# Decoder block on one core: the cross-attention's two halves as one unrolled program

## The chip, the cores and the metric

The kernel runs on one core of one Trainium2 chip. The metric is device time in microseconds (us). Three runs of the kernel before gave 2765.36, 2766.39 and 2767.1 us; the median is 2766.39 us.

## The reference

The program is one decoder block for 32 batches of 112 tokens with 512 channels, all float32. It adds three sublayers to `x`, each fed with a layer norm of `x`: windowed self-attention, cross-attention to a context, and a mixture of eight experts. The change touches the second.

```python
# text 32 x 112 x 512, context 32 x 375 x 256, 16 query heads, 8 key/value heads of 128
q = (text @ Wq).reshape(B, 112, 16, 128)      # Wq 512 x 2048
k = (ctx @ Wk).reshape(B, 375, 8, 128)        # Wk 256 x 1024
v = (ctx @ Wv).reshape(B, 375, 8, 128)        # each k, v head serves two query heads
attn = softmax(mask(q k^T / sqrt(128)))
out = (attn v).reshape(B, 112, 2048) @ Wo     # Wo 2048 x 512
x = x + out
```

## The kernel before

The program is four stages one after the other, with a barrier between them: `window_attention` (self-attention, which also writes the normalised, transposed text `h2T`), `cross_attention` for half 0, `cross_attention` for half 1, and `expert_ffn`. A half is 8 query heads and 4 key/value heads. Half 0 adds its part of the output to `x1` and writes `x1_half`; half 1 adds to that and writes `x2`.

Each float32 matrix product is made of three products in the format fp32r: an operand is split into a high part (ScalarE copies it, rounding) and a low part (VectorE subtracts the high part from the source), and `PASSES` multiplies high by high, high by low and low by high. So every result that TensorE makes for a later product is emptied from PSUM twice, by ScalarE and then by VectorE.

The products that feed the attention are called fills, and each has a letter. C transposes 128 context channels of a batch. K makes the keys of one key head of a batch (6 matmuls of 376 columns). V makes the values of a batch for 128 context rows (6 of 512 columns, three V fills a batch). Q makes queries of two heads for two batches (two groups of 12 matmuls of 224 columns). O multiplies the attention output of a batch with Wo (24 matmuls of 512 columns, 112 rows of output). Fills go through three PSUM banks in turn.

A step is one key head of one batch, with its two query heads. A turn is two batches, so eight steps, and a half has 16 turns. The first and last turn are written out; the 14 between are a hardware loop (`Fori`) on each engine. The order of all work is written out by hand in the list `FULL`, which gives each of the eight steps some of the fills, so that the steps are alike in TensorE work: no step has fewer than two or three fills except the two that have an O. On TensorE (L1461 on) a step `s` is: scores of `s`, transposes of the normalised probabilities of `s-1`, an O fill if there is one, the product of probabilities and values (pv) of `s-2`, and the other fills.

The softmax of a step goes round the engines. VectorE adds the mask and takes the maximum (`maxima`, L1279), GpSimd makes the bias from it (L1127), ScalarE takes the exponential and the sum (`exps`, L1199), VectorE inverts the sum (`inverses`, L1305 and L1308), GpSimd multiplies the probabilities (L1135), TensorE transposes them (L1436), and ScalarE and VectorE split them into `pT` (`probsT`, L1177 and L1286), which has room for two steps. The pv result in the one bank `ps_o` is split into `oT` (`out`, L1184 and L1294). Every engine works strictly in its written order.

The weights are staged: each 128 x 512 piece is loaded into free room (`stage`, `probs`, `sums`), then split. The text of two batches is loaded into `xf` and split into `xT` in one piece (L1192, L1261). The SyncE queue issues all the loads and stores.

Of the kernel before, what the change touches and what calls it, by code (L numbers as in the profile page):

```python
# [16 lines left out]
P = 128  # L17
# [99 lines left out]
def window_attention(nc, B, T, x, Wq, bq, Wk, bk, Wv, bv, Wo, bo, x1, h2T, slots, rest):  # L117
# [45 lines left out]
    with ExitStack() as stack:  # L163
# [51 lines left out]
        blank_made, blank_out = sem("blank_made"), sem("blank_out")  # L215
        x1_out = [sem(f"x1_out{s}") for s in range(TB)]
# [32 lines left out]
        with nc.Block() as block:  # L249
# [3 lines left out]
            def _(sp):  # L253
# [99 lines left out]
                sp.wait_ge(blank_out, 16 * (TURNS + 2))  # L353
                for s in range(TB):
                    sp.wait_ge(x1_out[s], 16 * TURNS)
# [106 lines left out]
            def _(act):  # L462
# [392 lines left out]
def cross_attention(nc, half, B, T, S, h2T, ctx, mask, Wq, Wk, Wv, Wo, base, result):  # L855


# [12 lines left out]
    H = 2 * G  # L870
    SE = S + S % 2
# [3 lines left out]
    assert 0 < SE - S or S % 2 == 0  # L875
    T2 = 2 * T
    TURNS = B // 2
    SCALE = float(1.0 / np.sqrt(D))
    mdt = mask.dtype

    LATE = [("Q", 0, 3), ("K", 0, 3), ("V", 0, 1), ("V", 0, 2)]
    FULL = [
        [("Q", 0, 3), ("K", 1, 0), ("V", 0, 1)],
        [("K", 0, 3), ("V", 0, 2), ("K", 1, 1), ("V", 1, 0)],
        [("O", 0, 1)],
        [("K", 1, 2), ("C", 0, 0), ("V", 1, 1), ("C", 0, 1)],
        [("K", 1, 3), ("V", 1, 2), ("Q", 0, 0)],  # L890
        [("K", 0, 0), ("Q", 0, 1)],
        [("K", 0, 1), ("Q", 0, 2)],
        [("O", 1, 0), ("K", 0, 2), ("C", 1, 0), ("V", 0, 0), ("C", 1, 1)],
    ]
    HEAD = [f for f in [("C", 0, 0), ("C", 0, 1)] + [("K", 0, g) for g in range(G)] + [("V", 0, c) for c in range(NKC)] +
            [("C", 1, 0), ("C", 1, 1)] + [("Q", 0, g) for g in range(G)] if f not in LATE]
    FIRST = [[f for f in fs if f != ("O", 0, 1)] for fs in FULL]
    LAST = [[f for f in fs if f[0] == "O" or f in LATE or (f[0] in "KV" and f[1] == 1)] for fs in FULL]
    TAIL = [("O", 0, 1)]
    NF = sum(map(len, FULL))  # L900
    NF0 = sum(map(len, FIRST))
    BASE = len(HEAD) + NF0 - NF
    flat = [f for fs in FULL for f in fs]
# [3 lines left out]
    def fills_until(turn, fill):  # L907

        if turn.reg is None and turn.at == -1:
            return HEAD.index(fill) + 1  # L910
# [1191 lines left out]
```

## Time and profile before

| | |
|---|---|
| profiled execution, span | 2765.4 us |
| median of three runs | 2766.39 us |
| TensorE matmul busy | 2589.5 us (94%) |
| VectorE busy | 1755.7 us (63%) |
| ScalarE busy | 1294.8 us (47%) |
| GpSimd busy | 1032.2 us (37%) |
| self-attention stage | 0 to 462 us |
| cross-attention, half 0 | 462 to 1474 us |
| cross-attention, half 1 | 1474 to 2487 us |
| expert stage | to 2765.4 us |

Busy shares are averages over stages with different limits. Matmuls are pipelined, so the time from the start of one block of matmuls to the start of the next is a better price for a block than its printed length, which reaches into the next block.

### The profile page before, as it was taken

The page shows a single profiled execution, that of the slowest core. Times are in us where ns is not written, and L with a number is a line of the kernel's source. Part 1 is how long each engine was busy: PE and PEld are TensorE (multiplying, and loading weights), DVE is VectorE, ACT ScalarE, POOL GpSimd, SP SyncE. Part 2 cuts the span into 40 slices and gives each one's busy share as a digit, 9 for nine tenths or more (in the row PEclk, how much of TensorE's full clock was granted, in tenths as well). Part 3 has the DMA queues.
Part 4 walks back from the last instruction along what each step waited for, and adds up shares of the span by engine and source line. Part 5 has one row for each costly group of instructions (what it writes and reads, how often), then busy time and mean ns, then how long its engine had stood idle before and what let it go on. Part 6 is the DMA issues. An engine that isn't in the chain of part 4 may idle for free. (4 is left out here: it accounts for less than half of the span.)

```text
span 2765.4 us, 56399 instructions
## 1 busy us (share of the span) xinstructions
PE 2589.5 (94%) x16770; PEld 2364.0 (85%) x16771; DVE 1755.7 (63%) x4862; ACT 1294.8 (47%) x3135; POOL 1032.2 (37%) x1426
## 2 busy tenths in 40 slices
PE   6899996899999999999996999999999999988688
PEld 5888886899999999999986899999999999978576
DVE  7888886656666665666664666665666665555466
ACT  4555554545545454554543545454554554441211
POOL 4334433333344433333341444333334344332422
PEclk9999998999999999999998999999999999995599
DMA  3223224111111111111113111111111111103654
GB/s 101 89 72 100 89 94 141 53 37 45 32 32 38 42 32 36 44 34 32 32 30 115 30 33 44 36 32 36 45 32 32 37 43 32 34 16 110 228 173 126
DMA packets 122050, 168.80 MB, mean 61 GB/s; under 512 B 20753, under 2 KB 69329, under 8 KB 121857
## 3 DMA queue, kind: packets, MB, share of 16 engines
q1 hardware_dynamic: 116944, 151.43, 18.3%
q0 software_dynamic: 5040, 16.58, 1.5%
q8 instruction: 33, 0.54, 0.1%
q14 instruction: 33, 0.26, 0.0%
HBM read 111.73 MB, written 56.23 MB: 61 GB/s over the span
## 5 line engine op out<-in xcount | busy, mean ns | idle before, releaser
L1135 POOL TENSOR_SCALAR x_probs<-x_probs,x_inv 112x376 f32<-112x376 f32 x512 | 652.5, 1285 | 237.2 <-DVE x_inv L1308 237.2
L1127 POOL TENSOR_SCALAR x_bias<-x_top 112x1 f32<-112x1 f32 x512 | 117.9, 230 | 977.5 <-DVE x_top L1279 976.5
L1392 PE MATMUL x_ps_f<-x_wo,x_oT 128*112 128x512 f32 x1536 | 374.8, 400 | 1.9 <-DVE x_oT L1294 1.9
L1392 PE MATMUL x_ps_f<-x_xT,x_wq 128*128 128x224 f32 x3072 | 365.8, 275 | 7.0 <-DVE x_xT L1261 7.0
L1392 PEld LDWEIGHTS x_ps_f<-x_xT,x_wq 128*128 128x128 f32 x3072 | 361.8, 193 | 10.4 <-issue 7.4
L1199 ACT ACTIVATE x_probs<-x_probs,x_bias 112x376 f32<-112x376 f32 x512 | 308.1, 604 | 64.1 <-POOL x_bias L1127 57.8
L1392 PEld LDWEIGHTS x_ps_f<-x_wo,x_oT 128*112 128x112 f32 x1536 | 265.3, 176 | 85.0 <-issue 2.2
L1452 PE MATMUL x_ps_o<-x_pT,x_v 128*128 128x224 f32 (+1 forms) x2304 | 315.6, 282 | 2.7 <-DVE x_oT L1294 2.7
L1424 PE MATMUL x_ps_s<-x_kT,x_qT 128*112 128x376 f32 x1536 | 311.4, 338 | 5.4 <-DVE x_wo L1244 5.4
L1392 PE MATMUL x_ps_f<-x_ctxT,x_wk 128*128 128x376 f32 x1536 | 312.7, 340 | 2.5 <-DVE x_ctxT L1250 2.5
L1392 PE MATMUL x_ps_f<-x_wv,x_ctxT 128*128 128x512 f32 (+1 forms) x1152 | 304.9, 400 | 0.0
L1177 ACT ACTIVATE x_pT<-x_ps_t 128x336 fp32r<-128x336 f32 x512 | 204.0, 449 | 206.0 <-PE x_ps_t L1436 206.0
L1452 PEld LDWEIGHTS x_ps_o<-x_pT,x_v 128*128 128x128 f32 (+1 forms) x2304 | 284.0, 193 | 9.6 <-issue 3.4
L1279 DVE CUSTOM_DVE_ANT_0 x_probs<-x_ps_s,x_mrow 112x376 f32<-112x376 f32 x512 | 259.8, 543 | 19.4 <-DVE x_mrow L1266 17.2
L1392 PEld LDWEIGHTS x_ps_f<-x_ctxT,x_wk 128*128 128x128 f32 x1536 | 262.4, 193 | 6.2 <-issue 3.2
L1424 PEld LDWEIGHTS x_ps_s<-x_kT,x_qT 128*112 128x112 f32 x1536 | 253.7, 175 | 12.9 <-DVE x_wo L1244 5.7
L1286 DVE TENSOR_TENSOR x_pT<-x_ps_t,x_pT 128x336 fp32r<-128x336 f32 x512 | 235.4, 500 | 9.3 <-ACT x_pT L1177 7.1
L1392 PEld LDWEIGHTS x_ps_f<-x_wv,x_ctxT 128*128 128x128 f32 (+1 forms) x1152 | 208.7, 187 | 36.3
L1250 DVE TENSOR_TENSOR x_v<-x_ps_f,x_v 128x512 fp32r<-128x512 f32 (+1 forms) x192 | 132.7, 691 | 151.1 <-ACT x_v L1169 151.0
L1250 DVE TENSOR_TENSOR x_qT<-x_ps_f,x_qT 128x448 fp32r<-128x448 f32 x128 | 79.9, 624 | 225.8 <-ACT x_qT L1169 225.8
L1184 ACT ACTIVATE x_oT<-x_ps_o 128x224 fp32r<-128x224 f32 x256 | 87.8, 343 | 278.2 <-PE x_ps_o L1452 278.2
L1436 PE MATMUL x_ps_t<-x_ident,x_probs 112*128 112x112 f32 x1536 | 192.4, 260 | 11.0 <-POOL x_probs L1135 11.0
(194 smaller groups left out, 3876.0 us busy)
## 6 DMA issues: line engine op xcount, KB each, us to landing
x_ctxn<-in_ctx_dram SPq DMA_DIRECT2D x64, 256.0 KB
x_xf<-h2T SPq DMA_DIRECT2D x32, 448.0 KB, 4.2
m_rows<-slots SPq DMA_DIRECT2D x35, 258.0 KB, 2.9
slots<-w_blank SPq DMA_DIRECT2D x8, 1032.0 KB, 5.2
m_hn<-in_L_ffn_W_dram SPq DMA_DIRECT2D x32, 256.0 KB, 4.9
x_ctxn<-in_ctx_dram SPq DMA_DIRECT2D x64, 119.0 KB
w_xa<-in_x_dram SPq DMA_DIRECT2D x32, 224.0 KB, 3.0
w_xr<-in_x_dram SPq DMA_DIRECT2D x32, 224.0 KB, 3.2
```

The lines of the kernel that those rows point to most:

```text
L1127: pool.tensor_scalar(bias[:, m:m + 1], top[:, m:m + 1], -0.1 * NEG, -SCALE, ALU.max, ALU.mult) \
L1135: pool.tensor_scalar(probs[0:T, m, 0:SE], probs[0:T, m, 0:SE], inv[:, m:m + 1], None, ALU.mult).then_inc(normed, 1)
L1177: act.activation(pT[:, s % 2, HI, :, h * T:(h + 1) * T], ps_t[h][:, 0:NKC * T].rearrange("p (c t) -> p c t", c=NKC), ACT.Copy).then_inc(pT ...
L1184: act.activation(oT[:, HI, 2 * g:2 * g + 2, odd * T:(odd + 1) * T], ps_o[:, 0:T2].rearrange("p (h t) -> p h t", h=2), ACT.Copy).then_inc(o ...
L1199: act.activation(probs[0:T, m, 0:SE], probs[0:T, m, 0:SE], ACT.Exp, bias=bias[:, m:m + 1], scale=SCALE, accum_out=total[:, m:m + 1]).then_ ...
L1250: dve.tensor_tensor(dst[LO], src, dst[HI].bitcast(F32), ALU.subtract).then_inc(fill_done, 1)
L1279: dve.tensor_tensor_reduce(out=probs[0:T, m, 0:SE], in0=ps_s[h][0:T, 0:SE], in1=mrow[:, s // 4, :], scale=1.0, scalar=-3.0e38, op0=ALU.add ...
L1286: dve.tensor_tensor(pT[:, s % 2, LO, :, h * T:(h + 1) * T], ps_t[h][:, 0:NKC * T].rearrange("p (c t) -> p c t", c=NKC), pT[:, s % 2, HI, : ...
L1392: last = pe.matmul(o, w, x, start=m == 0, stop=m == len(jobs) - 1)
L1424: last = pe.matmul(ps_s[h][0:T, 0:SE], qT[:, a, 2 * g + h, odd * T:(odd + 1) * T], kT[:, b_, g, :], start=m == 0, stop=m == 2)
L1436: last = pe.transpose(ps_t[h][:, c * T:(c + 1) * T], probs[0:T, n % 4, c * P:(c + 1) * P], ident[0:T, 0:T])
L1452: last = pe.matmul(ps_o[:, 0:T2], w, x, start=m == 0, stop=m == len(jobs) - 1)
```

## The change

Both halves become one `cross_attention` call, with every step written out in the program and no hardware loop: 64 batches (32 for each half) of 4 steps, 256 steps.

- Q fills make one query head for four batches at once: 12 matmuls of 448 columns. All eight of a group of four batches are issued in the last batch of the group before, two in each step.
- O fills work on 128 consecutive tokens and not on one batch: 28 tiles a half, 24 matmuls of 512 columns each with 128 rows of output. `oT` is a ring of 256 tokens. An O fill is issued in the third step (g = 2) of the batch after the one with its last token. Four batches of each half have none.
- The split, transposed context of each batch in half 0 is also stored to device memory (`ctxs`, 32 pieces of 128 x 1504 float32) and in half 1 loaded from there, so half 1 has no C fills.
- The three V fills of a batch stand together in its second step (g = 1); `v` and `pT` have room for one batch and one step, where they had two.
- A K fill of the next batch stands in every step; in half 0 two C fills stand in the fourth step (g = 3).
- TensorE's step is now: scores of `i`, K, C and O fills, pv of `i-2`, V and Q fills, and last the probability transposes of `i-1`. ScalarE and VectorE split `pT` of `i-2` at the start of step `i`. ScalarE copies K and C before `exps`.
- The text is split in four pieces, one a step, in the second batch of each group of four. The weights are loaded straight into the low half of their tile and split there, in pieces of 128 x 512 or 128 x 1024; those of half 1 are split in steps of the running program.
- The four weight matrices are copied in device memory (`own`) by four DMAs, issued from ScalarE's queue ahead of the first turn of the self-attention.

```diff
-        [("Q", 0, 3), ("K", 1, 0), ("V", 0, 1)],
-        [("K", 0, 3), ("V", 0, 2), ("K", 1, 1), ("V", 1, 0)],
-        [("O", 0, 1)],
...
+    def early_fills(i):
+        b, g = divmod(i, G)
+        out = [("K", b + 1, g)] if b + 1 < NB else []
+        if g == 3 and b + 2 < B:
+            out += [("C", b + 2, 0), ("C", b + 2, 1)]
+        if g == 2 and b in TILE_OF:
+            out.append(("O", TILE_OF[b], 0))
         return out
+    def late_fills(i):
+        b, g = divmod(i, G)
+        out = [("V", b, c) for c in range(NKC)] if g == 1 else []
+        if b % QUAD == QUAD - 1 and b + 1 < NB:
+            out += [("Q", b // QUAD + 1, 2 * g + h) for h in range(2)]
+        return out
...
-        pT = sb("pT", [P, 2, 2, NKC, T2], F32R)
+        pT = sb("pT", [P, 2, NKC, T2], F32R)
...
+                def keep_ctxT(b):
+                    sp.wait_ge(fill_done, until(("C", b, 1)))
+                    sp.dma_start(ctxs[b], ctxT[:, b % 2].rearrange("p a c s -> p (a c s)").bitcast(F32)) \
+                        .then_inc(ctx_out[b % 2], 16)
...
+                for i in range(STEPS):          # VectorE
+                    if i >= 2:
+                        probsT(i - 2)
+                    if i % G == 0:
+                        mask_row(i // G)
+                    maxima(i)
+                    for p in splits_at(i):
+                        split(p)
+                    for f in early_fills(i):
+                        if f[0] != "O":
+                            fill(f)
+                    inverses(i)
+                    if x_piece(i) is not None:
+                        split_x(x_piece(i), i % G)
+                    for f in early_fills(i):
+                        if f[0] == "O":
+                            add(f)
+                    if i >= 2:
+                        out(i - 2)
+                    for f in late_fills(i):
+                        fill(f)
...
+                for i in range(STEPS):          # TensorE
+                    scores(i)
+                    for f in early_fills(i):
+                        fill(f)
+                    if i >= 2:
+                        pv(i - 2)
+                    for f in late_fills(i):
+                        fill(f)
+                    if i >= 1:
+                        probsT(i - 1)
...
+                for n, (dst, src) in enumerate(copies):
+                    act.dma_start(dst, src).then_inc(copied[n], 16)
...
-    for half, (base, result) in enumerate(((x1, x1_half), (x1_half, x2))):
-        cross_attention(nc, half, B, T, S, h2T, ctx_1024, mask, xattn_Wq, xattn_Wk, xattn_Wv, xattn_Wo, base, result)
+    cross_attention(nc, B, T, S, h2T, ctx_1024, mask, *own, x1, x1_half, x2)
```

## Rows read from the trace of the kernel before

**Rows 1.** The page: busy time by engine, and TensorE's granted clock in 40 slices.
```profile
PE 2589.5 (94%) x16770; PEld 2364.0 (85%) x16771; DVE 1755.7 (63%) x4862; ACT 1294.8 (47%) x3135; POOL 1032.2 (37%) x1426
PEclk9999998999999999999998999999999999995599
```

**Rows 2.** Timeline of TensorE, one turn: start us, length us, engine, line, operation.
```profile
1001.03 1.20 PE L1424 MATMUL x_ps_s<-x_kT,x_qT 128*112 128x376 f32 x6
...
1002.58 5.82 PE L1392 MATMUL x_ps_f<-x_wo,x_oT 128*112 128x512 f32 x24
1008.24 1.16 PE L1452 MATMUL x_ps_o<-x_pT,x_v 128*128 128x224 f32 x9
...
1010.78 1.24 PE L1452 MATMUL x_ps_o<-x_pT,x_v 128*128 128x224 f32 x9
1011.86 1.20 PE L1392 MATMUL x_ps_f<-x_ctxT,x_wk 128*128 128x376 f32 x6
1012.90 0.48 PE L1373 MATMUL x_ps_f<-x_ident,x_ctxn 128*128 128x128 f32 x3
1013.14 1.63 PE L1392 MATMUL x_ps_f<-x_wv,x_ctxT 128*128 128x512 f32 x6
...
1019.99 2.83 PE L1392 MATMUL x_ps_f<-x_xT,x_wq 128*128 128x224 f32 x24
1022.66 1.19 PE L1424 MATMUL x_ps_s<-x_kT,x_qT 128*112 128x376 f32 x6
...
1060.40 1.56 PE L1392 MATMUL x_ps_f<-x_wv,x_ctxT 128*128 128x512 f32 x6
1061.80 1.20 PE L1424 MATMUL x_ps_s<-x_kT,x_qT 128*112 128x376 f32 x6
```

**Rows 3.** Timeline of TensorE, the same step of the first turn in each half.
```profile
536.47 1.19 PE L1424 MATMUL x_ps_s<-x_kT,x_qT 128*112 128x376 f32 x6
...
1546.82 1.19 PE L1424 MATMUL x_ps_s<-x_kT,x_qT 128*112 128x376 f32 x6
```

**Rows 4.** Timeline of the other engines, the softmax of one step.
```profile
1023.98 0.54 DVE L1279 CUSTOM_DVE_ANT_0 x_probs<-x_ps_s,x_mrow 112x376 f32<-112x376 f32 x1
...
1024.18 0.79 ACT L1177 ACTIVATE x_pT<-x_ps_t 128x336 fp32r<-128x336 f32 x2 [0.78 <-PE x_ps_t L1436]
...
1024.91 0.92 DVE L1286 TENSOR_TENSOR x_pT<-x_ps_t,x_pT 128x336 fp32r<-128x336 f32 x2
1024.96 0.61 ACT L1199 ACTIVATE x_probs<-x_probs,x_bias 112x376 f32<-112x376 f32 x1
...
1026.16 0.34 ACT L1184 ACTIVATE x_oT<-x_ps_o 128x224 fp32r<-128x224 f32 x1
1026.26 2.48 POOL L1135 TENSOR_SCALAR x_probs<-x_probs,x_inv 112x376 f32<-112x376 f32 x2 [0.88 <-DVE x_inv L1308]
```

**Rows 5.** Timeline of VectorE, the mask row of a batch and the maximum behind it.
```profile
1016.51 0.34 DVE L1266 TENSOR_SCALAR x_mrow<-x_mraw 112x375 f32<-112x375 uint8 x1
...
1017.11 0.55 DVE L1279 CUSTOM_DVE_ANT_0 x_probs<-x_ps_s,x_mrow 112x376 f32<-112x376 f32 x1 [0.26 <-DVE x_mrow L1266]
```

**Rows 6.** The instructions on the tile xT: count, nanoseconds min/median/max.
```profile
L1261 DVE TENSOR_TENSOR x_xT<-x_xf,x_xT x32: 1081/1092/1094, 488.2 to 2380.6; 128x896 fp32r<-128x896 f32 x32
```

**Rows 7.** Timeline of TensorE, a step of the last turn, which has no fills.
```profile
1448.13 1.19 PE L1424 MATMUL x_ps_s<-x_kT,x_qT 128*112 128x376 f32 x6
1450.22 0.51 PE L1436 MATMUL x_ps_t<-x_ident,x_probs 112*128 112x112 f32 x3 [0.90 <-POOL x_probs L1135]
...
1452.96 2.08 PE L1424 MATMUL x_ps_s<-x_kT,x_qT 128*112 128x376 f32 x6
```

**Rows 8.** Timeline of TensorE: transposes after two like waits, and an O fill behind another.
```profile
107.99 0.60 PE L758 MATMUL w_ps_f<-w_ident,w_h 112*128 112x112 f32 x4 [1.98 <-DVE w_xr L680]
...
377.49 1.00 PE L758 MATMUL w_ps_f<-w_ident,w_h 112*128 112x112 f32 x4 [1.98 <-DVE w_xr L680]
...
2466.52 7.26 PE L1392 MATMUL x_ps_f<-x_wo,x_oT 128*112 128x512 f32 x24
```

More of the change, by code:

```diff
@@ L946, in cross_attention, with split_all, x_piece @@
+    assert len(SPLITS) == HALVES * sum(PIECES.values())
+    def split_all(kind, half):
+        return max(SPLIT_NO[(kind, half, n)] for n in range(PIECES[kind])) + 1
+    def x_piece(i):
+        b, g = divmod(i, G)
+        return b // QUAD + 1 if b % QUAD == 1 and b // QUAD + 1 < NB // QUAD else None
+    ctxs = nc.dram_tensor("x_ctxs", [B, P, 2 * CC * SE], F32, kind="Internal").ap()
     with ExitStack() as stack:
         def sb(name, shape, dt=F32):
[L948 removed]
@@ L1187, in split_x, with out @@
-                def split_x(turn):
-                    act.wait_ge(x_in, turn.count(16, 16))
-                    if not (turn.reg is None and turn.at == 0):
-                        act.wait_ge(fill_ready, made(turn.before(), ("Q", 0, G - 1)))
-                    act.activation(x2[:, HI], xf[:], ACT.Copy).then_inc(x_hi, 1)
-                def exps(turn, s):
+                def out(i):
+                    b, g = divmod(i, G)
+                    act.wait_ge(pv_ready, i + 1)
+                    rows = ps_o[:, 0:T2].rearrange("p (h t) -> p h t", h=2)
+                    for t0, t1, at in pieces_of(b):
+                        last = act.activation(oT[:, HI, 2 * g:2 * g + 2, at:at + t1 - t0], rows[:, :, t0:t1], ACT.Copy)
+                    last.then_inc(o_hi, 1)
@@ L1343, in _ @@
-                turn_of(Turn(TURNS - 1))
-                last = Turn(TURNS - 1)
-                probsT(last, 7)
-                out(last, 6)
-                out(last, 7)
-                for n, f in enumerate(TAIL):
-                    before = BASE + NF * (TURNS - 1) + len(flatl) + n
-                    add(last, f, before, before % 3)
+                for p in FIRST_SPLITS[0]:
+                    split(p)
+                for f in HEAD[0:4]:
+                    fill(f)
+                for c in range(KC):
+                    split_x(0, c)
@@ L1352, in _ @@
+                for i in (STEPS - 2, STEPS - 1):
+                    probsT(i)
+                    out(i)
+                add(TAIL)
             @block.tensor
@@ L1360, in weights, with product @@
                         seen[0] = n
-                def fill(turn, f, before, b, fed):
-                    kind, odd, n = f
-                    if not (isinstance(before, int) and before < 3):
-                        pe.wait_ge(fill_done, before - 2)
-                    for s, value in fed:
-                        pe.wait_ge(s, value)
-                    out = ps_f[b]
+                def product(out, jobs):
+                    for m, (w, r) in enumerate(jobs):
+                        last = pe.matmul(out, w, r, start=m == 0, stop=m == len(jobs) - 1)
+                    return last
```

744 lines of the change are left out of this document (351 added, 393 removed).

## The prediction

> **What bounds the kernel.** I read the page first: TensorE is busy 94% of the span, the next engine 63%, and the granted clock is near its full 2.4 GHz in all slices but those of the expert stage [rows 1]. Then the timeline of one turn of the cross-attention. The reader is to see that no matmul block in it names a releaser: block follows block, and the turn lasts 1061.80 - 1001.03 = 60.8 us of TensorE work [rows 2]. 32 turns are 1945 us, so seven tenths of the span is TensorE's own instruction stream. There a removed matmul is removed time, as long as the other engines keep up. The third view is the passage between the halves: like points of the two lie 1546.82 - 536.47 = 1010.4 us apart, while 16 turns are 972.8 us, so 37.6 us go to the passage (drain, barrier, weights, first context, refill) [rows 3].
>
> The price of a block is the distance from its start to the next start [rows 2]: scores and probability transposes together 1.55 us, O 5.66, pv 1.08, K 1.04 (and so the scores, six matmuls of the same 376 columns, 1.04 too, and the transposes 0.51), C 0.24, V 1.40, Q 2.67 for 24 matmuls. The sum starts from the profiled execution, whose span of 2765.4 us is also its time; the median is 1.0 us above.
>
> **What is removed.**
> Q: 64 batches had 64/2 x 4 fills of 24 matmuls, 3072 at 2.67/24 = 111 ns, 341.8 us. After, 1536 of 448 columns. Nothing of this length and format is in the rows. The neighbours are 376 columns at 1.04/6 = 173 ns and 512 at 1.40/6 = 233 ns; on the line between them 448 lies at 205 ns, and this is nearer to the truth than either end. 1536 x 0.205 = 314.9 us: 26.9 us less. By the ends it would be 76 us less, or 16 more.
> The row says that two matmuls of 224 columns (222 ns) cost more than one of 448 by interpolation. The Trainium skill gives a reason (TensorE: Matmul & The Clock Gate, section LDWEIGHTS): a weight load takes its columns over 1.2 GHz, 107 ns for 128, more than the 93 ns in which 224 columns stream, so the load sets the pace; the 111 ns measured agree. By the same page's gap rule 448 columns would take 189 ns, and the Q saving would be 51 us; but that rule gives 159 ns for 376 columns where the row has 173, so I keep the row.
> O: 64 fills become 56, with 128 instead of 112 rows at the same columns. V has 128 rows and 233 ns a matmul, O 5.66/24 = 236, so the row count is free: 8 x 5.66 = 45.3 us less.
> C: half 1 loses 64 fills of 0.24 us, 15.4 us. Their bounds are 0 (if something else holds the step) and this.
> The passage between halves goes: 37.6 us. Its successors are weight splits in running steps, priced below. The first prologue and last drain stay; the prologue trades V fills for all Q fills, and I put its change at 0, between -8 and +8 (three V or Q fills).
> So far 2765.4 - 26.9 - 45.3 - 15.4 - 37.6 = 2640 us.
>
> **What is added: thin steps.** Before, every step had 5.6 us or more. Now a step has scores, K, pv and transposes, 1.04 + 1.04 + 1.08 + 0.51 = 3.67 us; V adds 4.2 in g = 1, O 5.7 in g = 2, Q 4.9 in each step of every fourth batch. Steps g = 3 and the next batch's g = 0 have nothing beyond 3.67 (in half 0, C adds 0.5 to g = 3).
> Against this stands a loop that does not run through TensorE's length: with one `pT`, VectorE splits the probabilities of i-2, then takes the maxima of i, ScalarE takes the exponentials, then copies `oT`, then starts the next `pT`. In rows: split 0.92; from maximum to first exponential 1024.96 - 1023.98 = 0.98; to the `oT` copy 1026.16 - 1024.96 = 1.20; that copy 0.34; the high part of the next split, 0.45 with the handover: 3.9 us [rows 4]. In g = 0 the mask row and its wait add 0.34 + 0.26 = 0.60 [rows 5]: 4.5 us against 3.67.
> Laid out from the scores of g = 3 at 0 (half 1): TensorE does pv of g = 1 at 2.08 with `pT` ready at 1.5, a slack of 0.5. VectorE's maxima come at 1.4 to 2.4; the exponentials wait for the K copy until 2.7; the `oT` copy is at 4.0, the next split at 4.8 to 5.7, so pv of g = 2 can start at 5.8, and TensorE arrives at 5.75. Then mask and maxima to 7.3, exponentials at 7.2 to 8.5, the split at 9.3 to 10.2: pv of g = 3 starts at 10.3, TensorE was there at 9.45. It idles 0.9 us. V fills then restore the slack. Behind the waiting pv stand only TensorE's own fills, so the idle time is lost.
> Where the batch has text pieces (each half of 1.09, 0.55 us on VectorE and about as much on ScalarE between `exps` and `out` [rows 6]), the idle time is 1.4; two of a group's four transitions have this. One after a Q batch has 0.7, one into a Q batch 0.1. That is 3.6 us a group of four batches, in half 0 4.5 with the C copies ahead of `exps` (0.3 each on three). 8 x 3.6 + 8 x 4.5 = 65 us. The eight batches without O have a third thin step, 0.8 us each: 6 us. Weight splits of 128 x 1024 (1.2 us on VectorE) stand in 14 steps, about half of them thin: 9 us. In sum 80 us, from 0 (all slack holds) to about 110 (a start 0.7 us worse at each of 48 transitions).
> That thin steps do stall can be seen in the drain: a step without fills lasts 1452.96 - 1448.13 = 4.8 us and waits for GpSimd [rows 7]. GpSimd's multiplication (2.48 us for two [rows 4]) now has a step more until its transposes, which stand last; by the layout they are ready 0.4 us or more before TensorE asks.
>
> **Other additions.** SyncE stores 32 and loads 32 pieces of 770 KB; a load is asked for three steps ahead, 13 us, and hides behind O and K (8 us where there is no O). If it doesn't, up to 4 us at 4 places. The weight copies, 10.5 MB, run in the self-attention, where no turn waits for a DMA; I take 3 us, near 0 for that reason; the upper end is the 37.6 us of the passage, which holds every wait for weights that the rows have. Unrolling I put at 0: first and last turns are written out before too, and their blocks have the looped turns' distances.
> Sum: 2640 + 80 + 3 = **2723 us**, 1.6% less than 2765.4.
>
> **Rivals.**
> No thin-step stalls: TensorE's stream still sets the pace everywhere, 2640 + 3 = 2643 us. For it: VectorE's whole work in a turn is under two thirds of it. Against: the loop of 3.9 to 4.5 us is longer than 3.67. Range 2635 to 2690.
> The clock, on the other side: an idle time of 1.98 us was followed in one turn by transposes of 0.60 us, in another by 1.00, slowed to 1.2 GHz, and an O fill behind the drain's waits took 7.26 us instead of 5.82 [rows 2, 8]. Each fall costs about 1.5 us. My idle times are 0.7 to 1.4 us, two per group in a row. If every one of the 56 transitions and O-less batches lets the clock fall, 2723 + 56 x 1.5 = 2807 us; from 28 falls on the kernel is slower than before. Against it: the first of the two waits of 1.98 us passed without a fall, and mine are shorter.
> Q matmuls at the 512-column price (233 ns): 43 us more, 2766, no change or slower. For it: each matmul needs its own 128-column weight load whatever its length. Against: 376 columns cost 60 ns less than 512.
>
> **Chances.** Forecast (2690 to 2758) 0.57; no stalls 0.24; clock 0.13; dear Q or several small costs 0.06. The measurement can tell 0.2%, 5.5 us, from no change. Faster takes the first two and some of the last: 0.83; within 0.2%: 0.04; slower 0.13. The range 2640 to 2775 leaves out the deep end of the clock case and the best prologue; the forecast's own range is 2690 to 2758.
>
> **What would show it.** A turn's worth of work (two batches) without stalls should be 58.5 us in half 0 and 57.5 in half 1. Q blocks start 2.46 us apart. The waits list should name VectorE's `pT` or `oT` as releaser of pv, about 65 us in all, in g = 0 and g = 1 and never in the fourth batch's later steps; V and O steps wait for nothing. At the half's change no gap over 2 us. If pv waits for nothing, the stall step is wrong; if the granted clock falls regularly, the clock rival is right; if DMA of `ctxT` is named, the reload is not hidden.

## The result

The changed kernel takes 2676.22 us (median of 4 runs, 2672.47 to 2677.2); the kernel before, beside it, 2766.74 us. The ratio is 0.9669, interval 0.9655 to 0.9682. The forecast was 2723 us: the direction was right, but the gain is 90.5 us and not 43. The time lies below the forecast's own range (2690 to 2758 us) and inside the range of its rival without stalls. Ratios in this document leave out two slow runs, one of the kernel before (2960.26 us) and one of e7_c_again (10168.72 us). The profiled execution has a span of 2673.7 us against 2765.4.

The page of the changed kernel first: busy time by engine, and the granted clock in 40 slices, against [rows 1].

```profile
PE 2490.9 (93%) x14850; PEld 2264.3 (85%) x14851; DVE 1732.6 (65%) x4899; ACT 1240.8 (46%) x3183; POOL 1027.4 (38%) x1424
PEclk9999999899999999999999999999999999985599
```

TensorE lost 98.6 us of busy time and stays the bound; the clock row is as before. Where the 91.7 us of the spans come from: the first matmul of the cross-attention is at 474.93 us (475.57 before), the first transpose of the expert stage (tile `m_a`) at 2411.14 (2500.02 before), and what lies behind that takes 262.6 us (265.4 before). So 88.2 us come from the cross-attention, 2.8 from the expert stage, 0.6 from the start. The prologue ahead of the first scores is 10.7 us longer (474.93 to 512.04 us, before 475.57 to 501.97), because it holds the Q fills of four batches; they are in the Q term below, and its printed idle time is the same (7.0 us, before 7.4).

The timeline of TensorE in half 0 of the changed kernel (start us, length us, engine, line, operation, idle time before and its releaser), from the last Q block of a group of four batches on. It answers to [rows 2].

```profile
865.15 1.25 PE L1370 MATMUL x_ps_s<-x_kT,x_qT 128*112 128x376 f32 x6
866.24 1.19 PE L1370 MATMUL x_ps_f<-x_ctxT,x_wk 128*128 128x376 f32 x6
867.27 1.16 PE L1370 MATMUL x_ps_o<-x_pT,x_v 128*128 128x224 f32 x9
...
868.78 1.26 PE L1370 MATMUL x_ps_s<-x_kT,x_qT 128*112 128x376 f32 x6
869.88 1.19 PE L1370 MATMUL x_ps_f<-x_ctxT,x_wk 128*128 128x376 f32 x6
871.18 1.26 PE L1370 MATMUL x_ps_o<-x_pT,x_v 128*128 128x224 f32 x9
872.28 4.36 PE L1370 MATMUL x_ps_f<-x_wv,x_ctxT 128*128 128x512 f32 x18
...
888.21 0.81 PE L1382 MATMUL x_ps_f<-x_ident,x_ctxn 128*128 128x128 f32 x6
888.78 1.24 PE L1370 MATMUL x_ps_o<-x_pT,x_v 128*128 128x224 f32 x9
...
895.12 1.19 PE L1370 MATMUL x_ps_f<-x_ctxT,x_wk 128*128 128x376 f32 x6
897.46 1.26 PE L1370 MATMUL x_ps_o<-x_pT,x_v 128*128 128x224 f32 x9 [1.15 <-DVE x_pT L1294]
...
905.40 5.60 PE L1370 MATMUL x_ps_f<-x_wo,x_oT 128*128 128x512 f32 x24
910.84 1.16 PE L1370 MATMUL x_ps_o<-x_pT,x_v 128*128 128x224 f32 x9
...
919.45 1.26 PE L1370 MATMUL x_ps_o<-x_pT,x_v 128*128 128x224 f32 x9 [0.53 <-DVE x_pT L1294]
...
923.74 1.27 PE L1370 MATMUL x_ps_o<-x_pT,x_v 128*128 128x224 f32 x9 [0.39 <-DVE x_pT L1294]
```

Three things are to be seen. The prices, start to start: K 867.27 - 866.24 = 1.03, O 910.84 - 905.40 = 5.44, both C fills 888.78 - 888.21 = 0.57; medians over half 0 are 4.20 for the 18 V matmuls and 4.87 for a Q block of 24. A thin step lasts 868.78 - 865.15 = 3.63 us. And only three steps of these four batches have a printed wait: g = 1 of the second batch (897.46) and g = 0 and g = 1 of the third (919.45, 923.74). The same three places wait in the other groups (in the last one g = 0 does not); in half 1 the four batches without an O fill wait in g = 3 too. Behind the Q fills the row at 871.18 prints no wait, but it is late: it starts 1.30 us behind its K (869.88), where a pv that does not wait starts 1.03 behind it (867.27). So it is in all 15 batches that follow a Q batch, by 0.18 to 0.27 us in 13 of them; in the other two, with more work for VectorE, the wait is printed.

The waits list of TensorE for the steady part, 560 to 2370 us (engine, line, tile, releaser: us in total, times, longest):

```profile
PE x_ps_o L1370 <- DVE x_pT L1294: 37.9, 53, 1.9
```

Over the whole span it is 43.9 us in 60 waits. The printed idle time is about 0.16 us less than what a wait adds from start to start (897.46 - 895.12 - 1.03 = 1.31 against 1.15), so the loss in printed waits is 43.9 + 60 x 0.16 = 53.5 us. Two more things belong to the sum. Five of the waits (6.0 us) are the drain of the last batch, and the kernel before has such waits too; the 13 late starts without a print add 2.7 us. That leaves 50.2 us for the thin steps. And a pv that was late takes 1.10 us to the next block (872.28 - 871.18) where the others behind K take 1.00, another 7 us for 68 of them, which are not in the 50.2.

### The profile page after: what moved, and what is told of

It is laid out like the page before. It is cut to its first block and busy times, and to the rows that moved or that the text cites. A ratio compares the mean times of both kernels' runs of the same rounds, so it can differ in the third digit from the quotient of the medians.

```text
span 2673.7 us, 46237 instructions
## 1 busy us (share of the span) xinstructions
PE 2490.9 (93%) x14850; PEld 2264.3 (85%) x14851; DVE 1732.6 (65%) x4899; ACT 1240.8 (46%) x3183; POOL 1027.4 (38%) x1424
## 5 line engine op out<-in xcount | busy, mean ns | idle before, releaser
L1165 POOL TENSOR_SCALAR x_probs<-x_probs,x_inv 112x376 f32<-112x376 f32 x512 | 638.1, 1256 | 251.8 <-DVE x_inv L1315 251.8
L1159 POOL TENSOR_SCALAR x_bias<-x_top 112x1 f32<-112x1 f32 x512 | 128.3, 251 | 897.6 <-DVE x_top L1287 890.7
L1370 PE MATMUL x_ps_o<-x_pT,x_v 128*128 128x224 f32 (+1 forms) x2304 | 309.8, 279 | 44.6 <-DVE x_pT L1294 43.9
L1370 PE MATMUL x_ps_f<-x_xT,x_wq 128*128 128x448 f32 x1536 | 323.8, 367 | 4.5 <-issue 4.5
L1370 PE MATMUL x_ps_s<-x_kT,x_qT 128*112 128x376 f32 x1536 | 322.6, 345 | 1.5 <-DVE x_top L1287 1.5
L1370 PE MATMUL x_ps_f<-x_wo,x_oT 128*128 128x512 f32 x1344 | 316.4, 391 | 1.0 <-DVE x_oT L1303 1.0
L1370 PEld LDWEIGHTS x_ps_f<-x_xT,x_wq 128*128 128x128 f32 x1536 | 286.9, 189 | 27.6 <-issue 4.7
L1370 PEld LDWEIGHTS x_ps_f<-x_wo,x_oT 128*128 128x128 f32 x1344 | 253.2, 189 | 50.1 <-issue 1.2
L1370 PE MATMUL x_ps_f<-x_wv,x_ctxT 128*128 128x512 f32 (+1 forms) x1152 | 279.8, 396 | 0.2 <-DVE x_kT L1264 0.2
L1185 ACT ACTIVATE x_kT<-x_ps_f 128x376 fp32r<-128x376 f32 x256 | 124.0, 485 | 261.6 <-PE x_ps_f L1370 261.2
L1201 ACT ACTIVATE x_oT<-x_ps_o 128x224 fp32r<-128x224 f32 (+6 forms) x352 | 93.5, 294 | 262.7 <-PE x_ps_o L1370 262.7
```

What stands on the lines that cost most here:

```text
L1159: pool.tensor_scalar(bias[:, m:m + 1], top[:, m:m + 1], -0.1 * NEG, -SCALE, ALU.max, ALU.mult) \
L1165: pool.tensor_scalar(probs[0:T, m, 0:SE], probs[0:T, m, 0:SE], inv[:, m:m + 1], None, ALU.mult).then_inc(normed, 1)
L1185: act.activation(dst[HI], src, ACT.Copy).then_inc(fill_hi, 1)
L1201: last = act.activation(oT[:, HI, 2 * g:2 * g + 2, at:at + t1 - t0], rows[:, :, t0:t1], ACT.Copy)
L1370: last = pe.matmul(out, w, r, start=m == 0, stop=m == len(jobs) - 1)
```

## The experiments

Each ratio is to the kernel before measured beside it (its medians there: 2782.3, 2768.2, 2780.7 and 2780.0 us). In all but the second of these four comparisons the part behind the first `m_a` block takes 275 to 278 us, and not 262 as in the first comparison. The stage column is free of what lies around: the time from the first scores block of the cross-attention to the first `m_a` block, in the profiled execution. In the changed kernel it is 2411.14 - 512.04 = 1899.1 us.

| run | ratio, interval | stage us | against 1899.1 |
|---|---|---|---|
| e1_spread_keys | 0.9753 [0.9737, 0.9769] | 1920.5 | +21.4 |
| e2_exp_first | 0.9871 [0.9855, 0.9888] | 1956.0 | +56.9 |
| e3_mask_early | 0.9628 [0.9610, 0.9647] | 1889.4 | -9.7 |
| e4_o_112_rows | 0.9675 [0.9659, 0.9691] | 1900.5 | +1.4 |
| e5_q_224 | 0.9780 [0.9764, 0.9797] | 1926.5 | +27.4 |
| e7_c_again | 0.9756 [0.9738, 0.9775] | 1918.2 | +19.1 |
| e9_pv_keys | 0.9530 [0.9512, 0.9548] | 1861.1 | -38.0 |
| e10_balanced | 0.9544 [0.9525, 0.9563] | 1865.4 | -33.7 |
| e12_text_moved | 0.9589 [0.9573, 0.9604] | 1875.5 | -23.6 |
| e13_keys_in_g3 | 0.9669 [0.9653, 0.9686] | 1899.7 | +0.6 |
| e14_mask_text | 0.9568 [0.9548, 0.9589] | 1869.9 | -29.2 |
| e15_mask_text_c | 0.9634 [0.9612, 0.9655] | 1886.9 | -12.2 |
| e6_before_copies | 1.0000 [0.9991, 1.0009] | | |
| e11_before_pitch | 0.9992 [0.9982, 1.0002] | | |

### The terms of the sum

**e5_q_224**

```diff
-  last = product(out[:, 0:T4], [(wq..., xT[:, b_, c, :]) ...])
+  for t in range(0, T4, T2):
+      last = product(out[:, t:t + T2], [(wq..., xT[:, b_, c, t:t + T2]) ...])
```

> Q fills for four batches as now, but each in two groups of 12 matmuls of 224 columns. Theory 1 (224 columns are paced by the weight load at 111 ns, 448 cost 203 ns): 1536 x (0.222 - 0.203) = 30 us more, 2706 us. Rival (the gain is not in the matmuls but in fewer and larger fills): 2676 us.

Timeline of TensorE in that run, a Q block and its successor:

```profile
953.10 5.52 PE L1370 MATMUL x_ps_f<-x_xT,x_wq 128*128 128x224 f32 x48
958.45 0.74 PE L1434 MATMUL x_ps_t<-x_ident,x_probs 112*128 112x112 f32 x6
```

48 matmuls in 5.35 us are 111 ns each, as before the change; 24 of 448 columns take 4.87. 60 of the 64 blocks lie in the stage, the other four in the prologue; 60 by 0.48 are 29 us, and the stage is 27.4 longer. The Q term is right: 203 ns a matmul where the interpolation gave 205. That 224 columns cost no less than 111 ns agrees with the weight load as the limit (the Trainium skill, TensorE: Matmul & The Clock Gate, section LDWEIGHTS, gives 107).

**e4_o_112_rows** and **e11_before_pitch** ask why an O block costs 5.44 us and not 5.66.

```diff
-  last = product(out[:], [(oT[:, a, h, slot:slot + P], wo[:, b_, h, :])
+  last = product(out[0:T], [(oT[:, a, h, slot:slot + T], wo[:, b_, h, :])
```

> O fills load 112 columns of oT as weights and make 112 rows instead of 128 (the last 16 tokens of each tile are left out, so the sums of those are not updated). In the traces 24 matmuls of an O fill start 5.44 us apart with 128 rows, 5.66 with 112 before. Theory 1 (the row count of the stationary operand makes the difference): O takes 5.66 us again, 56 x 0.22 = 12 us more, about 2688 us. Rival (the difference comes from something else, as the place of the fill or where its operands lie): 2674 to 2678 us.

```diff
-        oT = sb("oT", [P, 2, H, T2], F32R)      # the kernel before
+        oT = sb("oT", [P, 2, H, 256], F32R)
```

> The kernel before, with oT 256 tokens apart for each head and not 224; nothing else. Theory (the distance in memory between the heads' operands sets the price of an O matmul): an O block of 24 goes from 5.66 to 5.50 us, and the kernel is 64 x 0.16 = 10 us faster, ratio 0.996. Rival (it is the place: in the kernel before the O fill stands behind transposes, in the changed one behind a K fill): 5.66 us, ratio 1.000.

TensorE's timeline, an O block and its successor, first with 112 rows, then in the kernel before with the wider `oT`, then in e10_balanced, where O stands behind C:

```profile
905.85 5.68 PE L1370 MATMUL x_ps_f<-x_wo,x_oT 128*112 128x512 f32 x24
911.36 1.16 PE L1370 MATMUL x_ps_o<-x_pT,x_v 128*128 128x224 f32 x9
```

```profile
1003.52 5.75 PE L1392 MATMUL x_ps_f<-x_wo,x_oT 128*112 128x512 f32 x24
1009.11 1.16 PE L1452 MATMUL x_ps_o<-x_pT,x_v 128*128 128x224 f32 x9
```

```profile
898.31 5.73 PE L1376 MATMUL x_ps_f<-x_wo,x_oT 128*128 128x512 f32 x24
903.88 1.16 PE L1376 MATMUL x_ps_o<-x_pT,x_v 128*128 128x224 f32 x9
```

No single cause holds the 0.22 us. Median block before 5.65; with the wider `oT` 5.59; behind a K fill but with 112 rows 5.50; with 128 rows 5.44; with 128 rows behind transposes 5.54 to 5.57. So some 0.06 is the memory distance (or where the tiles behind the wider `oT` then lie, which moved with it), 0.1 to 0.13 the neighbour, 0.06 the rows; that these add up is taken from the three pairs and was not run as one. Both theories of e11 were too simple: the block got 0.06 cheaper, not 0.16, and the 3.8 us that this makes in 64 blocks are within what the ratio can tell. On e4 the rival was right that the row count is not the cause of most.

**e7_c_again** and **e6_before_copies**

```diff
-        if g == 3 and b + 2 < B:
+        if g == 3 and b + 2 < NB:        # C fills in half 1 too
...
-                            if half:
-                                pe.wait_ge(ctxT_in[at % 2], 16 * ((at - B) // 2 + 1))
-                            else:
-                                pe.wait_ge(fill_done, until(("C", at, 1)))
+                            pe.wait_ge(fill_done, until(("C", at, 1)))
```

> The changed kernel, but half 1 transposes the context again (C fills in g = 3 as in half 0) and neither stores nor loads the transposed context. Theory (the store and reload cost nothing, and TensorE's C fills are worth their length): half 1 gets 32 x 0.57 = 18 us less the two first batches' share it already had, 17 to 18 us, of which the waits of half 1 hide little; ratio 0.972 to 0.974. Rival (C in g = 3 falls into the waits of thin steps): 5 to 10 us, 0.970. Rival (the reload by DMA has a cost that the waits list does not name): no slower than the changed kernel.

19.1 us longer in the stage, where 32 x 0.57 = 18.2. The transposes cost their length, and the store and reload nothing that can be measured. The total ratio is a little above the range expected (0.9756).

```diff
+                for n, (dst, src) in enumerate(copies):      # in the kernel before
+                    act.dma_start(dst, src).then_inc(copied[n], 16)
```

> The kernel before with the four copies of the weights in device memory, issued in the self-attention, and its two halves reading the copies. Theory (the self-attention's last matmul moved from 461.4 to 463.4 us by the copies): 2 to 3 us longer, ratio 1.001. Rival (they are hidden, the 2 us were another placement of the traces): 1.000. If the second stage's weights come faster from a copy than from the input, the passage gets shorter, and the kernel is faster by up to 5 us: 0.998.

No difference. The self-attention ends 0.9 us later (2 us in the changed kernel), but the cross-attention's first matmul waits for its context anyway and starts at 475.45 us, where it started at 475.57 without the copies. The 3 us of the forecast are 0.

### The stalls of the thin steps

**e9_pv_keys** takes the wait away by taking other data:

```diff
-  pe.wait_ge(pT_lo, 2 * i + 2)
+  pe.wait_ge(fill_done, until(("K", min(b + 1, NB - 1), g)))
...
-  product(ps_o[:, 0:T2], [(v[...], pT[0:rows, b_, c, :]) ...])
+  product(ps_o[:, 0:T2], [(v[...], kT[0:rows, b_, g, 0:T2]) ...])
```

> pv multiplies the values with a part of the next batch's keys in place of pT, so that TensorE's pv never waits for the split of the probabilities; every engine still does all of its work (the output is not the reference's). Theory (the stall term is the wait for pT and nothing else): the ratio falls by the 54 us of the waits, from 0.9675 to 0.948 (2637 on a chip where the kernel before takes 2782), and no other wait comes in. Rival A (the loop itself is longer than TensorE's thin steps, so the next instruction in it that TensorE needs, the transposes' wait for the split two heads back, or the oT split, waits instead): 0.957 to 0.965. Rival B (some of what the waits list names would be lost anyway): under 25 us gained.

TensorE's waits list there, same stretch:

```profile
PE x_ps_o L1370 <- DVE x_oT L1303: 13.3, 25, 1.5
```

38.0 us go; the rest comes back, nearly all of it as the wait for `oT`, 13.3 us in 25 waits, the next link of the same loop (the transposes wait 2.2 us for GpSimd's `probs`). So the listed waits were real losses. The ratio, 0.953, lies between the theory's 0.948 and rival A's 0.957 to 0.965: most of the wait is for the last piece of the loop, and the loop is too long without it as well.

**e1_spread_keys** and **e2_exp_first** were the first tries at it.

```diff
-        out = [("K", b + 1, g)] if b + 1 < NB else []
+        out = [("K", b + 1, 0)] if g == 3 and b + 1 < NB else [("K", b, 2)] if g == 0 and b else []
...
+        if g == 3 and b + 1 < NB:
+            out.append(("K", b + 1, 1))      # late, behind pv
+        if g == 0 and b:
+            out.append(("K", b, 3))
```

> The K fills of keys 1 and 2 leave the steps g = 1 and g = 2, which V and O make long, and stand in g = 3 and the next g = 0, so that these two steps have two K fills each (4.7 us of TensorE work) and g = 1, g = 2 none. Same work, other places. Theory 1 (thin steps are bound by the VectorE/ScalarE loop of 3.9 to 4.5 us, and nothing else waits): the 54 us that TensorE loses before pv fall to under 15 us, the time to about 2632 us (0.951 of before). Theory 2 (the loss belongs to single-buffered pT and v, whatever the length of the step): the waits stay or move to other steps, 2665 to 2680 us. Theory 3: VectorE and ScalarE get one more evacuation in just the steps in which they are late, and it gets worse: 2690 us or more.

```profile
925.75 1.26 PE L1374 MATMUL x_ps_s<-x_kT,x_qT 128*112 128x376 f32 x6
927.82 1.27 PE L1374 MATMUL x_ps_o<-x_pT,x_v 128*128 128x224 f32 x9 [0.82 <-DVE x_pT L1298]
```

The timeline shows why it got slower: the waits of g = 0 went (9.4 to 0.7 us), but g = 1 has only scores ahead of pv now, and the waits moved there (28.2 to 48.6 us, in all four batches of a group); over 560 to 2370 us there are 66 waits with 50.5 us, where there were 53 with 37.9.

```diff
+                    exps(i)
                     for p in splits_at(i):
                         split(p)
                     for f in early_fills(i):
                         if f[0] != "O":
                             fill(f)
-                    exps(i)
```

> ScalarE does the exponentials before it copies K and C, and VectorE the inverses before it subtracts them; all else as in the changed kernel. Theory 1 (the loop bounds the thin steps, and the copies of K and C stand in it in g = 3): the loop starts 0.3 us earlier in half 1 and 1.0 us earlier in half 0, so waits before pv shrink by 15 to 25 us in sum, mostly in half 0: 2650 to 2662 us. Rival (copies fall into idle time of ScalarE, or the loop is restarted by the wait for the bias): no change, 2672 to 2680 us.

ScalarE's wait for the bias, in the changed kernel and then here (both 560 to 2370 us):

```profile
ACT x_probs L1209 <- POOL x_bias L1159: 100.4, 120, 2.1
```

```profile
ACT x_probs L1209 <- POOL x_bias L1159: 424.8, 237, 3.1
```

In the changed kernel the K and C copies stand where ScalarE would wait for the bias. Behind `exps` they delay the `oT` copy, and the kernel got 56.9 us slower. The run moved VectorE's inverses as well, so the two engines' parts are not told apart. TensorE's waits for `pT` rose from 37.9 to 56.9 us, and 12.7 us of waits for K and C to leave their PSUM banks came in; the granted clock fell to half seven times between 540 and 1565 us, for 34 us together (some 15 us of the 56.9, by the price that a fall of 3.4 us has in the changed kernel, below; an estimate).

**e3_mask_early** and **e12_text_moved** shorten the loop one piece at a time.

```diff
-                    if i % G == 0:
-                        mask_row(i // G)      # between split and maxima of g = 0
...
+                    if i % G == 2 and i // G + 1 < NB:
+                        mask_row(i // G + 1)  # at the end of VectorE's g = 2
```

> The mask row of the next batch is made at the end of VectorE's work in g = 2, not between the split and the maxima of g = 0. Theory (each wait before pv is the excess of the loop split, maxima, exponentials, oT copy, next split over TensorE's thin step): the loop of g = 0 falls from 4.26 to 3.8 us, the wait behind it (0.5 to 0.6 us in most batches) goes or nearly goes; of about 54 us that the waits cost, 15 to 25 go: ratio to the kernel before 0.959 to 0.962, where the changed kernel has 0.967 to 0.9675. Rival (as with the moved keys: a removed wait comes back a step later, since the slack of TensorE isn't there): the waits only move, ratio 0.966 to 0.969.

9.7 us, less than the theory's 15 to 25. By the printed waits, those of g = 1 fall from 18.6 to 14.8 us in the second batches of the groups and from 7.3 to 2.4 in the third. Those of g = 0 in the third batches stay (8.4 and 8.8 us). And the mask row now stands ahead of the split of g = 3, and there, in the batches that have no O fill to cover it, the waits grow from 2.4 to 6.2 us. So the rival (a removed wait comes back elsewhere) holds for a part.

```diff
-        return b // QUAD + 1 if b % QUAD == 1 and b // QUAD + 1 < NB // QUAD else None
+        return b // QUAD + 1 if b % QUAD in (1, 2) and g in (1, 2) and b // QUAD + 1 < NB // QUAD else None
```

> The changed kernel with one thing moved: the four pieces of the text, which were split in the four steps of the second batch of a group, are split in g = 1 and g = 2 of the second and third batch, beside V and O fills. Theory (the pieces in g = 3 and g = 0 put 0.5 us on each engine into the loop of thin steps): the wait of about 1.1 us before pv in g = 1 of the second batch (16 of them, 18.6 us in the waits list) falls to 0.5 or less; 8 to 14 us earlier, ratio 0.963 to 0.965. Rival (the pieces lie in ScalarE's and VectorE's idle time and the wait there is that of the first thin pair since the Q fills): under 3 us, 0.967.

23.6 us: more than expected, and some 1.5 of it is a fall of the clock that the changed kernel has and this run has not (see the rivals below). What the pieces do can be read in the other engines' timeline of the changed kernel. First a step g = 0 without one: split, mask row, maximum, exponential, `oT` copy, next split.

```profile
865.96 0.91 DVE L1294 TENSOR_TENSOR x_pT<-x_ps_t,x_pT 128x336 fp32r<-128x336 f32 x2
866.79 0.35 DVE L1275 TENSOR_SCALAR x_mrow<-x_mraw 112x375 f32<-112x375 uint8 x1
867.30 0.55 DVE L1287 CUSTOM_DVE_ANT_0 x_probs<-x_ps_s,x_mrow 112x376 f32<-112x376 f32 x1 [0.17 <-DVE x_mrow L1275]
...
868.22 0.61 ACT L1209 ACTIVATE x_probs<-x_probs,x_bias 112x376 f32<-112x376 f32 x1 [0.27 <-POOL x_bias L1159]
...
869.42 0.39 ACT L1201 ACTIVATE x_oT<-x_ps_o 128x96 fp32r<-128x96 f32 x2
...
870.22 0.91 DVE L1294 TENSOR_TENSOR x_pT<-x_ps_t,x_pT 128x336 fp32r<-128x336 f32 x2
```

Then one with a piece of the text (`x_xT`):

```profile
774.26 0.92 DVE L1294 TENSOR_TENSOR x_pT<-x_ps_t,x_pT 128x336 fp32r<-128x336 f32 x2
...
777.89 0.56 ACT L1178 ACTIVATE x_xT<-x_xT 128x448 fp32r<-128x448 f32 x1
...
778.48 0.63 DVE L1258 TENSOR_TENSOR x_xT<-x_xT 128x448 fp32r<-128x448 f32 x1
...
779.32 0.91 DVE L1294 TENSOR_TENSOR x_pT<-x_ps_t,x_pT 128x336 fp32r<-128x336 f32 x2
```

The loop is 870.22 - 865.96 = 4.26 us without and 779.32 - 774.26 = 5.06 us with the piece. The same step of the second batch takes 4.33 in e12_text_moved, where it has no piece. So a piece costs 0.73 and not 0.55, because it stands on ScalarE ahead of the `oT` copy and then on VectorE ahead of the `oT` split. Moved beside V and O, the 16 waits of g = 1 in the second batch fall from 18.6 to 7.8 us, and those of g = 0 in the third from 8.4 to 0.5.

**e13_keys_in_g3** moves only fills, **e10_balanced** all three things, **e14_mask_text** mask row and text, **e15_mask_text_c** these and the C fills.

```diff
-        out = [("K", b + 1, g)] if b + 1 < NB else []
-        if g == 3 and b + 2 < B:
+        out = [("K", b + 1, k) for k in ((0,), (1,), (), (2, 3))[g]] if b + 1 < NB else []
+        if g == 2 and b + 2 < B:
```

> The changed kernel with only the order of fills changed: the third and fourth K fill of the next batch both stand in g = 3 ahead of pv, none in g = 2; the C fills of half 0 go from g = 3 to g = 2. Theory (waits are the excess of the loop over TensorE's work in the pair g = 3 and g = 0): that pair gets 1.03 us of work more that was beside O, so of 54 us of waits some 20 to 30 go; ratio 0.956 to 0.960, and what stays stands where the text is split. Rival (as when K was moved behind out): the waits stay or grow, 0.967 or more.

Nothing gained: the theory missed, and the rival's 0.967 is met within the interval. The reason is the best lesson of the study. Timeline of ScalarE and VectorE in half 1, the step g = 3 behind an O fill, in the changed kernel:

```profile
1724.79 0.92 DVE L1294 TENSOR_TENSOR x_pT<-x_ps_t,x_pT 128x336 fp32r<-128x336 f32 x2
...
1726.66 0.48 ACT L1185 ACTIVATE x_kT<-x_ps_f 128x376 fp32r<-128x376 f32 x1 [1.56 <-PE x_ps_f L1370]
1727.04 0.60 ACT L1209 ACTIVATE x_probs<-x_probs,x_bias 112x376 f32<-112x376 f32 x1
...
1728.93 0.92 DVE L1294 TENSOR_TENSOR x_pT<-x_ps_t,x_pT 128x336 fp32r<-128x336 f32 x2
```

and with the two K fills:

```profile
1724.02 0.92 DVE L1294 TENSOR_TENSOR x_pT<-x_ps_t,x_pT 128x336 fp32r<-128x336 f32 x2
...
1726.91 0.48 ACT L1185 ACTIVATE x_kT<-x_ps_f 128x376 fp32r<-128x376 f32 x1 [0.54 <-PE x_ps_f L1370]
1727.29 0.60 ACT L1209 ACTIVATE x_probs<-x_probs,x_bias 112x376 f32<-112x376 f32 x1
...
1729.19 0.92 DVE L1294 TENSOR_TENSOR x_pT<-x_ps_t,x_pT 128x336 fp32r<-128x336 f32 x2
```

ScalarE copies K ahead of the exponentials, so these wait until TensorE has finished the fill. The loop went from 4.14 to 5.17 us, by the 1.03 us that TensorE's step got longer. A fill whose copy stands in the loop gives no slack here. In half 0, where C left the step at the same time, the loop went from 4.89 to 5.17 us.

> The mask row as in the kernel with the early mask row; of the K fills of the next batch, the first and second stay in g = 0 and g = 1 ahead of pv, the third and fourth both stand in g = 3 ahead of pv (before: one in every step); the C fills of half 0 go from g = 3 to g = 2; the pieces of the text and of the weights for K and Q are split only in g = 1 and g = 2, where V and O fills are. Theory: the excess of the loop over the thin step of g = 3 is 4.7 against 3.9 us then, so the waits go nearly all: first matmul of the expert stage's m_a 40 to 50 us earlier than the 2412 of the changed kernel's copies, ratio 0.950 to 0.954. Rival (keys taken from g = 2 leave the wait to the step behind, as in the kernel with the spread keys): ratio 0.964 or more.

```diff
-        if b == B - 8 and g < CC:
-            return [("k", 1, g)]
-        if b == B - 3:
-            return [("q", 1, g)]
+        if b == B - 8 and 1 <= g <= CC:
+            return [("k", 1, g - 1)]
+        if B - 3 <= b < B - 1 and 1 <= g <= 2:
+            return [("q", 1, 2 * (b - B + 3) + g - 1)]
```

(with the diffs of e3, e12 and e13.) TensorE's waits list, same stretch:

```profile
PE x_ps_o L1376 <- DVE x_pT L1298: 10.5, 18, 1.8
PE x_ps_o L1376 <- issue: 2.7, 4, 0.7
```

This version beats both kernels: 2641.2 us, 0.9544 of the kernel before where the changed one has 0.9669; their intervals are apart. It is within 5 us of the kernel whose pv does not wait for `pT` at all. The four waits without a releaser ("issue") stand in the steps g = 2 of half 1 that have neither K nor O fill; their cause is open.

> The changed kernel with the early mask row and with the pieces of the text and of the weights for K and Q split only in g = 1 and g = 2; the K and C fills stand where the changed kernel has them. First matmul of m_a: 2411.1 in the changed kernel, 2400.8 with the mask row moved, 2385.9 with the text moved, 2412.3 with the K fills moved, 2378.2 with all of it. Theory (mask row and text are two pieces of the same loop, the K fills are worth nothing): 2411.1 - 10.3 - 25.2 - 1 or 2 for the weights = 2374 to 2376, ratio 0.952 to 0.954, no slower than with all three. Rival (K fills in g = 3 pay only once the loop is short): 2381 to 2385, ratio 0.956 to 0.958.

29.2 us, where the two alone add to 33.3. The first matmul of `m_a` is at 2384.7 and not at 2374 to 2376; 2.8 us of this lie in the prologue, whose end is at 514.80 and not 512.04. Part of the rest is the split of Wo in batch 33: its wait at 1498.47 us is 1.83 us (1.11 in e12), and the granted clock falls to half behind it for 3.4 us, as in the changed kernel and not in e12 or e10. Between e14 and e10 are 4.5 us. Without the fall of the clock some 3 are left for the order of the K and C fills, once the loop is short: the rival's mechanism, and its number (2381 to 2385) with the help of prologue and clock.

> The same with the C fills of half 0 in g = 2 ahead of the O fill instead of g = 3. Theory (C copies stand ahead of the exponentials in g = 3, 0.5 us of the loop; O behind C costs 0.1 us more, 28 times 0.09 = 2.5 us; and TensorE's 0.57 us leave the thin step): the two cancel, within 3 us of the kernel without it. Rival (the copies are in ScalarE's wait for the bias, so nothing is gained): 3 us or more slower.

17 us slower than e14: the theory missed, and the rival has the number but not the cause. The waits list names what neither had:

```profile
PE x_ps_f L1376 <- DVE x_kT L1268: 14.1, 25, 1.5
```

K, C, C and O are four fills in a row for three PSUM banks; the O fill takes K's bank and waits 0.51 us until VectorE has emptied it. In e10_balanced g = 2 has no K, and this wait is absent.

## Why the prediction was right in direction and wrong in size

Forecast and measurement, in us of the profiled executions:

| step of the prediction | forecast | measured | where from |
|---|---|---|---|
| Q in 448 columns | -26.9 | -30.1 | 341.8 - 64 x 4.87; e5 |
| O, 56 fills | -45.3 | -57.6 | 64 x 5.66 - 56 x 5.44; e4, e11 |
| C of half 1 | -15.4 | -12.5 | 128 fills at 0.24, then 32 pairs at 0.57; e7 |
| passage | -37.6 | -37.6 | taken whole: no gap at the half's change |
| thin-step stalls | +80 | +50.2 | waits list and late starts, without the drain; e9 |
| weight copies | +3 | 0 | e6 |
| expert stage, start | 0 | -3.4 | 262.6 against 265.4 and 0.6 |
| rest | 0 | -0.7 | what is left |
| sum | -42 | -91.7 | |

The last row but one is what is left when the others are added, and it is small because larger things cancel. Blocks whose work did not change got other neighbours. Scores behind transposes cost 1.10 us where most had 1.03 to 1.04 behind a fill, 11 us more over 256 steps. Against it, pv behind K or O costs 1.00 (1.10 if late) where it mostly had 1.08 behind transposes, 6 us less over all, and V no longer stands behind a C block (1.47 there, 1.40 elsewhere), 4 us less. The sum of the prediction had none of these.

**The failing step is the size of the stall term**: 80 us forecast, 50 measured, which is 30 of the 49 us by which the forecast missed; O is 12.3. Its mechanism was right. The waits list names VectorE's `pT` as the releaser of pv, as foretold, with 44 us and not 65 and in the steps foretold. The layout of the thin steps stands to 0.2 us, counted from the scores of g = 3 in half 1: the exponentials at 1727.04 - 1724.33 = 2.71, the split at 4.60, pv of g = 2 at 5.77 (foretold: 2.7, 4.8, 5.8).

```profile
1724.33 1.26 PE L1370 MATMUL x_ps_s<-x_kT,x_qT 128*112 128x376 f32 x6
...
1730.10 1.16 PE L1370 MATMUL x_ps_o<-x_pT,x_v 128*128 128x224 f32 x9
```

What failed is the list of transitions. Each group was given four: 1.4 us twice for the text, 0.7 behind a Q batch, 0.1 into one, and 0.9 more in half 0 for C. Measured from start to start in half 0, the two with text are 1.15 + 0.16 = 1.31 and 0.53 + 0.39 + 0.32 = 1.24 us, a little below, in part by luck: a plain transition costs less than the 0.9 that I took (below), and a piece of text more, 0.73 and not 0.5. The 0.7 is 0.2 to 0.3 (871.18, above): the Q fills of g = 3 stand behind pv, so the loop gets 4.87 us there for nothing and runs ahead, by more than I gave it. The 0.1 is 0. The C copies, 0.9, are 0.2 to 0.6 by the groups of the two halves: that they lie largely in ScalarE's wait for the bias fits e2, which took them out of it. The batches without O have 3 us of stalls, all in half 1, not 6; the weight splits (batches 24, 29 and 32 to 34) some 4, not 9. And the price of a plain transition is 0.64 us in e12 (32 waits, 15.4 us printed), since the loop of g = 0 is 4.26 us and not 4.5. In sum: text and C 39 us where 52 were foretold, behind a Q batch 3 where 11, into one 0 where 2, without O 2 where 6 (the third of its 3 us is a weight split's), weight splits 4 where 9, and 2 in the first two batches that nothing had foretold.

**The Q and O terms.** The interpolation was good to 2 ns. For O I took the row's price as the operation's own; place, memory distance and rows made it 0.22 us cheaper.

**The passage.** Its 37.6 us came back, as far as the timeline can tell. At the change of half the timeline of TensorE has only one wait between 1456 and 1475 us:

```profile
1472.04 1.26 PE L1370 MATMUL x_ps_o<-x_pT,x_v 128*128 128x224 f32 x9 [0.61 <-DVE x_pT L1294]
```

What the prediction put in its place, the weight splits, shows in the waits of batches 32 to 34, the longest of them 1.80 us (1498.30, below).

**The transfers.** On the page, the pieces of `ctxs` land 3.8 us (store) and 4.3 us (load) after their issue; no instruction waits for them.

```profile
x_ctxs<-x_ctxT SPq DMA_DIRECT2D x32, 752.0 KB, 3.8
x_ctxT<-x_ctxs SPq DMA_DIRECT2D x32, 752.0 KB, 4.3
```

**The rivals.** The clock rival had the right price and the wrong count. In the steps of the changed kernel the clock fell once, in batch 33, where Wo is split:

```profile
1498.30 2.12 PE L1370 MATMUL x_ps_o<-x_pT,x_v 128*128 128x224 f32 x9 [1.80 <-DVE x_pT L1294]
1500.21 5.10 PE L1370 MATMUL x_ps_f<-x_wv,x_ctxT 128*128 128x512 f32 x18
```

The granted clock is half (1.2 GHz) for 3.4 us from 1498.48 us; pv took 1.91 us and not 1.10, the V fills 4.95 and not 4.20, together 1.6 us where 1.5 were foretold. In 505 to 1470 us and 1502 to 2384 us it is 1.00, behind the waits of 1.0 to 1.4 us and also behind one of 1.92 us at 1376.75. A slice of the page is 67 us long and hides such a fall. Q at the price of 512 columns is refuted by e5's run and 4.87 us. "No stalls" had the nearer number (2643 against 2676; the forecast 2723) and the wrong mechanism: 50 us of stalls are there, and without them the span would be some 2623 us, 20 below this rival. Its number came near because it had two errors that partly cancel: it left out the stalls, and it had O, Q and the weight copies 18 us too dear.

**The work of two batches.** Foretold 58.5 us in half 0. A group of four with all its O fills lasts 122.1 us there, 2.6 of it waits; with an O fill less in every second group, half of the rest is 58.4. In half 1 it is 57.0 (119.1 us, 2.3 of it waits), foretold 57.5.

## What to carry to other kernels

Price a wait step by step along the list of what each engine does, and ask for each long fill whether it stands before or behind the waiting instruction: behind it, it feeds the loop slack for the next steps, and a copy of it ahead of the loop's own instruction takes that slack away (e13, e14 against e10). Before moving work into a thin step, look at the engine that empties it: where its copy stands in the loop, step and loop grow together. Small once-a-batch work (mask rows, pieces of the next operand) belongs beside the longest fill, not in an even spread: here this alone was worth 29 us (e14), where the stalls were 50. And a list of waits is a lower bound: compare the distances between blocks as well, for the late starts too short to be printed.

## What was not expected of the hardware

- The same 24 matmuls of 512 columns took 5.44 to 5.65 us, by neighbour, distance in memory and rows (0.06 to 0.13 us each). A block behind transposes is the dearer one: in the kernel before, scores cost 1.10 behind C transposes and 1.03 behind V or Q fills.
- A pv that waited, or was late by as little as 0.18 us, takes 1.10 us to the next block; one that was not takes 1.00. Behind K, in 560 to 2370 us, these are 63 of 64 late blocks (the other one ran at half clock) and 91 of 97 others.
- 10.5 MB of copies between places in device memory, beside a running stage, cost no measurable time (1.0000, interval 0.9991 to 1.0009).
- A program of 256 steps written out had no instruction stall that the profile shows: in 560 to 2370 us TensorE's waits list of the changed kernel has one entry, the `pT` above. (In e10 and e13 there are four waits of 0.7 us whose releaser is not named, in e1 seven.)
